# Attention prologue of a fused two-layer transformer kernel: fewer scores among the query/key blocks, the second stack's transfers interleaved, the last output tile in two halves

## The chip, the cores and the metric

One core of a Trainium2 chip runs the whole program. The metric is the device time of one execution in microseconds (us). Five things work side by side on a core: TensorE (PE in the profile; PEld is its loading of weights), VectorE (DVE), ScalarE (ACT), GpSimd (POOL) and SyncE (SP), whose queue here issues every transfer (SPq). They meet only at semaphores, and each does its instructions in program order. A median moved by under 0.2% can't be told from no change here.

## What is computed

Two blocks over 1024 tokens of width 512. The first (a state-space scan and a routed feed-forward) isn't touched. The second is attention with 32 heads of width 16 and a linear position bias, and a gated feed-forward with ternary weights. What matters, cut from the reference:

```
qkv = hidden_states @ w_attn + b_attn            # 1024 x 1536
scores = einsum('bqhd,bkhd->bhqk', q, k) * SCALE
scores = where(causal, scores + bias, -inf)
attn = softmax(scores)
out = einsum('bhqk,bkhd->bqhd', attn, v) @ w_proj + b_proj
...
inter = silu(gate) * up;  inter_q = trunc(clip(inter * 128, -128, 127))
down = einsum('bsi,hi->bsh', inter_q, w_down)
out = trunc(clip(down * 128, -128, 127));  x = x + gb * out
```

## The kernel before, in words

**Heads and stacks.** The heads go in eight groups of four. Queries and keys are computed in float32 and split into three bfloat16 parts each. A *stack* of a group holds these parts, and rows for the bias, one above the other, so that one bfloat16 matmul gives the exact score. There are three stack buffers; group g lies in `stack[g % 3]`.

**Query/key blocks.** `QK_ORDER` lists 16 blocks of 128 channels by 512 tokens. For block i TensorE does four float32 matmuls (L1123; the profile has two records for each), ScalarE copies the result to `qkf` (L746), VectorE makes the three parts `qkp` in four instructions (L1550 to L1553), and SP writes them to DRAM (`parts_dram`, L383). `qkp` has three buffers, so VectorE's block i waits for the write of block i-3. `qkf` has two.

**Loads of stacks.** `load_stack(g)` issues 14 loads: two for each of the six entries of TERMS (queries and keys) and two of position rows (`alibi`). All are issued by the helper at L321. SP issues stack 0 right after the write of block 4, once the writes of blocks 0 to 4 have landed, and stack 1 in one go after the write of block 6. The write of block 7 stands behind it in SP's queue. Blocks 0 to 4 hold all that both stacks need.

**Scores and maxima.** Before the softmax each row's extreme is found. `scores(n)` on TensorE makes one PSUM bank of scores (L1065: four heads of a 128x128 tile in four matmuls; L1068: one head by 512 keys). `maximum(n)` on VectorE reduces it to `mrow`: four masked reductions L1506 where the tile lies on the diagonal, otherwise one instruction, L1510 or L1513. The banks form a ring of three: score n waits until the maximum of the entry three before it is done. A group has 36 of them (SU). Scores run 48 (S_PRO) ahead of the attention loop, and these first 48 are made in two places: behind the last query/key blocks (`s_early(i)` says how many are done after block i), and between the steps of the values' projection (`s_steps(t, k)`). That projection, the V phase below, has 8 tiles of 4 steps, each step one matmul (two records of L1140). At the first score VectorE also copies a mask, `negT` (L1501), for which score 2 waits.

**The shift.** When group 0's 36 maxima are in, VectorE joins them (`rr`), GpSimd splits the result into parts (`rp`), TensorE transposes it (L1049, just before score 40), VectorE casts it (L1528) and SP loads it as three rows into the stack (`stack<-r`). `transposed_scores(0)`, the loop's first product (L1081), waits for these rows.

**The attention loop.** 288 steps, each with a score 48 ahead, a transposed score (L1081), ScalarE's exponential and, seven steps behind, the product with the values (L1101).

**The last stage.** The down projection has eight tiles of 128 tokens by 512 columns, 33 bfloat16 matmuls each (L1250). For a tile VectorE does nine dependent instructions (L1612, L1613, L1590 to L1593, L1595, L1616, L1618), ScalarE one (L807), and SP writes the tile out (L417). No other work is left then.

Of the kernel before, what the change touches and what calls it, by code (L numbers as in the profile page):

```python
# [29 lines left out]
EPS = 1e-5  # L30
QK_ORDER = ((0, 0), (4, 0), (1, 0), (0, 1), (4, 1), (5, 0), (1, 1), (5, 1),
            (2, 0), (6, 0), (3, 0), (7, 0), (2, 1), (6, 1), (3, 1), (7, 1))
S_QK = 9
QK_FIRST = 2
LEAD = 12
PV_LAG = 7
MAGIC = 12582912.0
HIGH = 3e38
TERMS = ((0, 0), (1, 0), (2, 0), (0, 1), (1, 1), (0, 2))
ATT_R = 3  # L40
ATT_A = 24
# [41 lines left out]
S_PRO = SU + LEAD  # L83
# [14 lines left out]
def program(nc, a, out):  # L98
    ctx = ExitStack()
    with ctx:  # L100
# [7 lines left out]
        x_tok = at("x_tok", 0, [P, NT, D])  # L108
# [91 lines left out]
        stack = [at("stack0", G_AT + 54, [P, 2, GH, T], BF16), at("stack1", F_AT + 22, [P, 2, GH, T], BF16),  # L200
                 at("stack2", G_AT + 32, [P, 2, GH, T], BF16)]
# [54 lines left out]
        def tile(t):  # L256
            return slice(t * P, (t + 1) * P)


        def s_early(i):  # L260
            return 0 if i < S_QK else (3 * (i - S_QK) + 4) // 2

        def s_steps(t, k):

            early = s_early(15)
            return early + (S_PRO - early) * (t * DC + k + 1) // (NT * DC)

        def qk_bank(i):
            return i if i < 4 else 4 + i % 4
# [49 lines left out]
        def _(sp):  # L319
            def load(dst, src, s):  # L320
                sp.dma_start(dst, src).then_inc(s, 16)  # L321
# [45 lines left out]
            load(bv[:], a["b_v"], S["bias1"])  # L367
            load(bpc[:], a["b_proj"].partition_broadcast(P), S["bias1"])

            def load_stack(g):  # L370
                def rows(part, first):
                    at_ = first + g * GH * HD
                    return parts_dram[part, at_:at_ + GH * HD, :].rearrange("(d h) t -> d (h t)", h=GH)

                for n, (qp, kp) in enumerate(TERMS):
                    load(stack[g % 3][n:ATT_K:ATT_W, 0, :, :], rows(qp, 0), stk[g % 3])
                    load(stack[g % 3][n:ATT_K:ATT_W, 1, :, :], rows(kp, D), stk[g % 3])
                load(stack[g % 3][ATT_W - 1:ATT_K:ATT_W, 1, :, :].bitcast(U16), a["alibi"][g][0:HD], stk[g % 3])
                load(stack[g % 3][ATT_K:ATT_S, 1, :, :].bitcast(U16), a["alibi"][g][HD:ATT_A], stk[g % 3])

            for i, (ob, h) in enumerate(QK_ORDER):
                sp.wait_ge(S["qk_split"], i + 1)
                sp.dma_start(parts_dram[:, ob * P:(ob + 1) * P, half(h)].rearrange("q p t -> p q t"), qkp[:, i % 3, :, :]) \  # L383
                  .then_inc(qk_wr[i % 3], 16)
                if i == 4:
                    for r in range(3):
                        sp.wait_ge(qk_wr[r], 16 * (2 if r < 2 else 1))
                    load_stack(0)
                if i == 6:
                    load_stack(1)  # L390
            for i in range(3):
                sp.wait_ge(qk_wr[i], 16 * len(range(i, 16, 3)))

# [18 lines left out]
            sp.wait_ge(S["ao_done"], 2 * NG)  # L412
            load(wd[:, 0:IC - 1, :], a["wd"][0:(IC - 1) * P, :].rearrange("(k p) n -> p k n", p=P), S["in_down"])
            load(wd[0:INTER - (IC - 1) * P, IC - 1, :], a["wd"][(IC - 1) * P:INTER, :], S["in_down"])
            for t in range(NT):
                sp.wait_ge(S["dn_done"], t + 1)
                sp.dma_start(out[tile(t), :], x_tok[:, t, :]).then_inc(S["out_dma"], 16)  # L417
            sp.wait_ge(S["out_dma"], 16 * NT)


        @block.gpsimd
# [114 lines left out]
        def _(act):  # L536
            n = [0]
# [6 lines left out]
            A_ = act.activation  # L544
# [214 lines left out]
            for F in range(NG * FU):  # L759
                g, f = F // FU, F % FU  # L760
# [5 lines left out]
                if on:  # L766
                    x = ps[:, 3 + F % 3, :].rearrange("p (n c) -> p n c", c=P)[:, on[0]:on[1] + 1:on[1] - on[0], :]
# [10 lines left out]
            for i in range(2 * IC):  # L778
                if i == 1:
                    ln_out(3, 1, 3, 4, (1,))  # L780
                ib, s = i % IC, i % 2
                M = min(P, INTER - ib * P)

                for part in range(3):
                    k = i - part
# [14 lines left out]
                if i >= 2:  # L800
                    act.wait_ge(S["f_out"], i - 1)
                A_(f_s[0:M, s, :], f_y[0:M, s, :], ACT.Sign).then_inc(S["f_sgn"], 1)
            for t in range(NT):
                act.wait_ge(S["dn_y0"], t + 1)
                if t >= 2:
                    act.wait_ge(S["dn_y"], t - 1)
                A_(f_s[:, t % 2, :], f_y[:, t % 2, :], ACT.Sign).then_inc(S["dn_sgn"], 1)  # L807


        @block.tensor  # L810
        def _(pe):
            mm = pe.matmul
# [156 lines left out]
            for m in range(N_ALL):  # L969
                h, s = m // NS, m % NS  # L970
# [143 lines left out]
            n = 0  # L1114
            for i, (ob, h) in enumerate(QK_ORDER):
# [18 lines left out]
            for t in range(NT):  # L1134
# [57 lines left out]
            for F in range(NG * FU):  # L1192
                g, f = F // FU, F % FU
# [34 lines left out]
            for i in range(2 * IC):  # L1228
# [3 lines left out]
                h, ib, s = i // IC, i % IC, i % 2  # L1232
                M = M_of(i)
# [9 lines left out]
            for t in range(NT):  # L1243
                pe.wait_ge(S["f_out"], IC * (t // 4 + 1))
                if t >= 4:
                    pe.wait_ge(S["dn_y"], t - 3)
                for k in range(IC):
                    M = M_of(k)
                    for part in range(3):
                        ins = mm(ps[:, 4 + t % 4, :], inter[0:M, k, tile(t)], wdp[0:M, part, k, :],  # L1250
                                 start=(k == 0 and part == 0), stop=(k == IC - 1 and part == 2))
                ins.then_inc(S["dn_mm"], 1)

# [2 lines left out]
        def _(v):  # L1256
            n = [0]

            def link(ins):
                n[0] += 1  # L1260
                ins.then_inc(S["dchain"], 1)
                v.wait_ge(S["dchain"], n[0])

            ts, tt, stt = v.tensor_scalar, v.tensor_tensor, v.scalar_tensor_tensor
# [323 lines left out]
            def trunc(y, s, M, sgn_sem, sgn_count, dst):

                link(ts(f_a[0:M, s, :].bitcast(I32), y.bitcast(I32), 0x7FFFFFFF, None, ALU.bitwise_and))  # L1590
                link(ts(f_m[0:M, s, :], f_a[0:M, s, :], MAGIC, None, ALU.add))
                link(stt(f_a[0:M, s, :], f_m[0:M, s, :], MAGIC, f_a[0:M, s, :], ALU.subtract, ALU.subtract))
                link(stt(f_m[0:M, s, :], f_a[0:M, s, :], 0.0, f_m[0:M, s, :], ALU.is_gt, ALU.subtract))  # L1593
                v.wait_ge(sgn_sem, sgn_count)
                return stt(dst, f_m[0:M, s, :], MAGIC, f_s[0:M, s, :], ALU.add, ALU.mult)  # L1595

            for i in range(2 * IC):
                h, ib, s = i // IC, i % IC, i % 2
# [9 lines left out]
            for t in range(NT):  # L1608
                s = t % 2
                v.wait_ge(S["dn_mm"], t + 1)  # L1610

                link(ts(f_y[:, s, :], ps[:, 4 + t % 4, :], -128.0, -128.0, ALU.mult, ALU.max))  # L1612
                ts(f_y[:, s, :], f_y[:, s, :], 127.0, None, ALU.min).then_inc(S["dn_y0"], 1)  # L1613
                v.wait_ge(S["dn_y0"], t + 1)
                link(trunc(f_y[:, s, :], s, P, S["dn_sgn"], t + 1, f_r[:, s, :]))
                tt(f_r[:, s, :], f_r[:, s, :], gb1[:], ALU.mult).then_inc(S["dn_y"], 1)  # L1616
                v.wait_ge(S["dn_y"], t + 1)
                tt(x_tok[:, t, :], x_tok[:, t, :], f_r[:, s, :], ALU.subtract).then_inc(S["dn_done"], 1)  # L1618
# [82 lines left out]
```

## Time and profile before

| | us |
|---|---|
| median of 3 runs | 903.29 (902.1 to 904.23) |
| the profiled execution, its own time | 903.27 |
| its span in the profile | 901.5 |
| PE busy | 850.0 (94%) |
| DVE busy | 742.8 (82%) |
| ACT busy | 472.0 (52%) |
| POOL busy | 308.9 (34%) |

The span is what the profile's records cover; the time is 1.77 us longer. Busy times of PE are sums of modelled lengths: a matmul's record is longer than the distance to the next, so the distance between two starts tells what one costs. The stage around the change runs from about 325 us (first query/key block) to 428 us (start of the attention loop); the last stage from 836 us to the end.

### The profile page before, as it was taken

The numbers are of one execution on the slowest core, as the hardware profiler recorded it, in microseconds if no ns is written. First come the engines' busy times: TensorE is split into PE (matmuls) and PEld (weight loads), VectorE is DVE, ScalarE is ACT, GpSimd is POOL, SyncE is SP. The second block draws the span as 40 slices with busy tenths as digits, with TensorE's granted clock in tenths as the row PEclk, the third lists the DMA queues.
The fourth block names the chain that finished last, engine by engine and source line by source line (L and its number), as shares of the span: only waits on it lengthen the run. The fifth ranks groups of instructions, "written<-read, shape, count | busy, mean of one in ns | idle before, by whom it ended". The sixth has DMA issues, their size and how long they took to land.

```text
span 901.5 us, 12080 instructions
## 1 busy us (share of the span) xinstructions
PE 850.0 (94%) x4031; PEld 401.3 (45%) x4031; DVE 742.8 (82%) x1589; ACT 472.0 (52%) x904; POOL 308.9 (34%) x342
## 2 busy tenths in 40 slices
PE   5999978999989999899999999999999999999996
PEld 3445424455437454444444444443344444444442
DVE  5689999999997875787999999995156899767777
ACT  4767654665652031111888888888624656333100
POOL 1057999999993100050122212212111433000000
PEclk9878999999999999999999999999999999999998
DMA  9300060300005005610322202200051000000011
GB/s 345 113 0 1 1 275 5 140 1 1 1 0 202 8 29 160 201 61 2 89 81 81 59 27 79 82 3 2 1 199 53 1 0 0 1 0 1 12 43 39
DMA packets 22136, 54.07 MB, mean 60 GB/s; under 512 B 6085, under 2 KB 12869, under 8 KB 19066
## 3 DMA queue, kind: packets, MB, share of 16 engines
q1 hardware_dynamic: 22074, 53.30, 17.1%
q8 instruction: 32, 0.52, 0.2%
q14 instruction: 30, 0.25, 0.1%
HBM read 44.70 MB, written 8.39 MB: 59 GB/s over the span
## 4 chain that ended last, share of the span: by engine, by line
PE 62%; DVE 4%; SPq 2%; POOL 1%; ACT 1%; issue 1%; DMA 1%; POOLq 0%; DVEq 0%
PE ps L1239 17%; PE ps L1101 8%; PE ps L1081 7%; PE ps L1250 6%; PE ps L1065 4%; PE ps L1068 4%; PE ps L1160 3%; PE ps L1009 3%; PE ps L1140 3%; PE ps L1123 2%; SPq L321 2%; PE ps L818 1%; POOL hC L482 1%; PE ps L1003 1%; PE ps L1110 1%
## 5 line engine op out<-in xcount | busy, mean ns | idle before, releaser
L482 POOL TENSOR_TENSOR hC<-hs,C_sb 128x512 f32<-128x512 f32 x128 | 160.7, 1274 | 51.4 <-ACT C_sb L701 30.7
L771 ACT ACTIVATE prob<-ps 128x512 f32<-128x512 f32 x288 | 157.8, 602 | 25.8 <-PE ps L1081 11.5
L989 PE MATMUL ps<-hC,identf 128*128 128x512 f32 x256 | 139.7, 650 | 13.2 <-POOL hC L482 12.2
L630 ACT ACTIVATE ps<-dtT,nA 128x512 f32<-128x512 f32 x128 | 88.2, 690 | 50.1 <-DVE hs L1394 46.6
L1081 PE MATMUL ps<-stack 123*128 123x512 bf16 (+3 forms) x384 | 108.5, 327 | 1.3 <-ACT prob L771 1.1
L520 POOL TENSOR_SCALAR_AFFINE_SELECT prob<-prob 128x256 f32<-128x256 f32 x96 | 39.2, 409 | 162.8 <-ACT prob L771 162.8
L1513 DVE TENSOR_REDUCE mrow<-ps 128x1 f32<-128x512 f32 x128 | 81.7, 682 | 6.3 <-PE ps L1068 4.3
L1101 PE MATMUL ps<-prob,V 128*32 128x512 f32 (+3 forms) x768 | 81.6, 498 | 0.7 <-POOL prob L520 0.7
L989 PEld LDWEIGHTS ps<-hC,identf 128*128 128x128 f32 x256 | 48.5, 204 | 72.8 <-POOL hC L482 53.1
L1239 PE MATMUL ps<-hT,wg 128*128 128x512 f32 (+1 forms) x176 | 79.1, 592 | 0.0
L1239 PE MATMUL ps<-hT,wu 128*128 128x512 f32 (+1 forms) x176 | 79.1, 592 | 0.0
L1394 DVE TENSOR_TENSOR_SCAN hs<-ps,dBx 128x512 f32<-128x512 f32 x64 | 77.7, 1214 | 1.2 <-ACT ps L630 1.2
L1372 DVE TENSOR_TENSOR dBx<-uT,ps 128x512 f32<-128x512 f32 x112 | 74.0, 662 | 3.8 <-PE ps L883 3.5
L1394 DVE TENSOR_TENSOR_SCAN hs<-ps,state,dBx 128x512 f32<-128x512 f32 x56 | 69.9, 1270 | 0.3 <-ACT ps L630 0.3
L1506 DVE CUSTOM_DVE_ANT_0 ps<-ps,negT 128x128 f32<-128x128 f32 x256 | 66.0, 321 | 3.3 <-PE ps L1065 2.0
L1510 DVE TENSOR_REDUCE mrow<-ps 128x4 f32<-128x512 f32 x96 | 63.2, 684 | 5.3 <-PE ps L1065 4.9
L1065 PEld LDWEIGHTS ps<-stack 120*128 120x128 bf16 x640 | 44.5, 97 | 48.6 <-issue 22.2
L1065 PE MATMUL ps<-stack 120*128 120x128 bf16 x640 | 61.6, 219 | 2.7 <-DVE mrow L1506 1.5
L1250 PE MATMUL ps<-wdp,inter 128*128 128x512 bf16 (+1 forms) x264 | 57.2, 379 | 0.0
L1123 PE MATMUL ps<-hT,wattn 128*128 128x512 f32 x128 | 56.6, 595 | 0.0
L1239 PEld LDWEIGHTS ps<-hT,wu 128*128 128x128 f32 (+1 forms) x176 | 33.0, 188 | 42.5 <-issue 42.5
L1239 PEld LDWEIGHTS ps<-hT,wg 128*128 128x128 f32 (+1 forms) x176 | 32.9, 188 | 42.0 <-issue 42.0
(202 smaller groups left out, 1334.8 us busy)
## 6 DMA issues: line engine op xcount, KB each, us to landing
stack<-parts_dram SPq DMA_DIRECT2D x96, 128.0 KB
wmod<-in_wmod SPq DMA_DIRECT2D x4, 1536.0 KB, 12.4
parts_dram<-qkp SPq DMA_DIRECT2D x16, 384.0 KB, 2.6
wmod<-in_wmod SPq DMA_DIRECT2D x4, 1024.0 KB, 10.5
wattn<-in_wattn SPq DMA_DIRECT2D x1, 3072.0 KB, 10.1
wg<-in_wg SPq DMA_DIRECT2D x1, 2752.0 KB, 11.0
wu<-in_wu SPq DMA_DIRECT2D x1, 2752.0 KB, 10.7
wd<-in_wd SPq DMA_DIRECT2D x1, 2560.0 KB, 11.1
```

Of the source, the lines that this page charges most:

```text
L482: pool.tensor_tensor(hC[:, c, :], hs[:, c, :], C_sb[:, m % 2, :], ALU.mult).then_inc(S["hc_done"], 1)
L630: A_(ps[:, DA_BANK + c % 2, :], dtT[:, c, half(h)], ACT.Exp, scale=nA[:, c * NS + s:c * NS + s + 1]).then_inc(S["da_done"], 1)
L771: A_(prob[:, u % 4, j, :], ps[:, 3 + F % 3, :], ACT.Exp, scale=-1.0).then_inc(S["exp_done"], 1)
L989: mm(ps[:, c, :], identf[:], hC[:, c, :], start=False, stop=(s == NS - 1), skip_group_check=True).then_inc(S["sum_done"], 1)
L1065: ins = mm(ps[:, bank, tile(j_)], qk[0:ATT_S, 0, j_, tile(i)], qk[0:ATT_S, 1, j_, tile(kb)], start=True, stop=True)
L1081: ins = mm(ps[:, bank, col:col + w], qk[0:ATT_ALL, 1, j, tile(kb)], qk[0:ATT_ALL, 0, j, q0:q0 + w], start=True, stop=not diag)
L1101: ins = mm(ps[32 * j:32 * j + 32, 6 + b, q0 % HALF:q0 % HALF + w], V[:, kb, g * GH + j, :], prob[:, U % 4, j, col:col + w], start=(kb == 0 ...
L1123: ins = mm(ps[:, qk_bank(i), :], wattn[:, k, ob * P:(ob + 1) * P], hT[:, k, half(h)], start=(k == 0), stop=(k == DC - 1))
L1239: ins = mm(ps[0:M, 2 * s + b, :], w[:, k, ib * P:ib * P + M], hT[:, k, half(h)], start=(k == 0), stop=(k == DC - 1))
L1250: ins = mm(ps[:, 4 + t % 4, :], inter[0:M, k, tile(t)], wdp[0:M, part, k, :], start=(k == 0 and part == 0), stop=(k == IC - 1 and part == 2))
L1394: v.tensor_tensor_scan(hs[:, c, :], ps[:, DA_BANK + c % 2, :], dBx[:, c, :] if c < mine else dB3[m % 2], init, ALU.mult, ALU.add).then_inc ...
L1513: v.tensor_reduce(mrow[:, 0, j, i:i + 1], ps[:, bank, :], AX, ALU.min).then_inc(S["m_done"], 1)
```

## The change

Three edits.

1. `S_QK` goes from 9 to 10 and `s_early` from (3(i-9)+4)/2 to i+1-10. After blocks 9 to 15 there used to be 2, 3, 5, 6, 8, 9 and 11 scores; now there are 0, 1, 2, 3, 4, 5 and 6. The five others go to the V phase: `s_steps` now gives no score after its first three steps (`V_AHEAD = 3`) and spreads 42 over the other 29, where it spread 37 over 32.
2. Stack 1 isn't loaded in one go after the write of block 6. Two of its loads follow each of the writes of blocks 6 to 12.
3. The last tile of the down projection is done as two halves of 256 columns, through all engines, to the write of the output.

```diff
-S_QK = 9
+S_QK = 10
+V_AHEAD = 3
...
+DOWN = [(t, 0, D) for t in range(NT - 1)] + [(NT - 1, 0, D // 2), (NT - 1, D // 2, D // 2)]
...
         def s_early(i):
-            return 0 if i < S_QK else (3 * (i - S_QK) + 4) // 2
+            return max(0, i + 1 - S_QK)
 
         def s_steps(t, k):
 
             early = s_early(15)
-            return early + (S_PRO - early) * (t * DC + k + 1) // (NT * DC)
+            return early + (S_PRO - early) * max(0, t * DC + k + 1 - V_AHEAD) // (NT * DC - V_AHEAD)
...
-                if i == 6:
-                    load_stack(1)
+                if 6 <= i < 6 + ATT_W:
+                    load_rows_of(1, i - 6)
...
-            for t in range(NT):
-                sp.wait_ge(S["dn_done"], t + 1)
-                sp.dma_start(out[tile(t), :], x_tok[:, t, :]).then_inc(S["out_dma"], 16)
+            for n, (t, c0, w) in enumerate(DOWN):
+                sp.wait_ge(S["dn_done"], n + 1)
+                sp.dma_start(out[tile(t), c0:c0 + w], x_tok[:, t, c0:c0 + w]).then_inc(S["out_dma"], 16)
...
-            for t in range(NT):
+            for n, (t, c0, w) in enumerate(DOWN):
                 pe.wait_ge(S["f_out"], IC * (t // 4 + 1))
-                if t >= 4:
-                    pe.wait_ge(S["dn_y"], t - 3)
+                if n >= 4:
+                    pe.wait_ge(S["dn_y"], n - 3)
                 for k in range(IC):
                     M = M_of(k)
                     for part in range(3):
-                        ins = mm(ps[:, 4 + t % 4, :], inter[0:M, k, tile(t)], wdp[0:M, part, k, :],
+                        ins = mm(ps[:, 4 + n % 4, 0:w], inter[0:M, k, tile(t)], wdp[0:M, part, k, c0:c0 + w],
                                  start=(k == 0 and part == 0), stop=(k == IC - 1 and part == 2))
...
-                link(ts(f_y[:, s, :], ps[:, 4 + t % 4, :], -128.0, -128.0, ALU.mult, ALU.max))
+                link(ts(y, ps[:, 4 + n_ % 4, 0:w], -128.0, -128.0, ALU.mult, ALU.max))
...
```

`load_rows_of(1, n)` issues the two loads of entry n, for n = 6 those of the position rows; `load_stack(g)` is now a loop over it. ScalarE's sign and VectorE's nine instructions of the down tiles get the width `w` in the same way.

How the instructions move. On TensorE, from the tenth query/key block to the fourth score of the V phase, before (in the kernel before L1123 is a query/key block, L1065 and L1068 scores, L1140 the V phase):

```order
L1123 MATMUL ps<-hT,wattn 128x512 x32
L1129 MATMUL ps<-identb,negm 128x128
L1065 MATMUL ps<-stack_126 128x128 x8
L1123 MATMUL ps<-hT,wattn 128x512 x4
L1065 MATMUL ps<-stack_126 128x128 x4
L1123 MATMUL ps<-hT,wattn 128x512 x4
L1065 MATMUL ps<-stack_126 128x128 x8
...
L1065 MATMUL ps<-stack_126 128x128 x8
L1140 MATMUL ps<-wattn,hT 128x512
L1068 MATMUL ps<-stack_126 128x512
L1140 MATMUL ps<-wattn,hT 128x512
L1068 MATMUL ps<-stack_126 128x512
```

And now (L1132 is the block, L1074 and L1077 the scores, L1149 the V phase):

```order
L1132 MATMUL ps<-hT,wattn 128x512 x36
L1138 MATMUL ps<-identb,negm 128x128
L1074 MATMUL ps<-stack_126 128x128 x4
L1132 MATMUL ps<-hT,wattn 128x512 x4
L1074 MATMUL ps<-stack_126 128x128 x4
L1132 MATMUL ps<-hT,wattn 128x512 x4
...
L1074 MATMUL ps<-stack_126 128x128 x4
L1149 MATMUL ps<-wattn,hT 128x512 x4
L1074 MATMUL ps<-stack_126 128x128 x4
L1149 MATMUL ps<-wattn,hT 128x512
L1074 MATMUL ps<-stack_126 128x128 x4
```

The first scores come one block later and singly, and four steps of the V phase go ahead of its first score. On SP, the transfers behind the load of stack 0 (stack_127 is stack 1), before:

```order
L383 DMA parts_dram<-qkp 128x3x512 x2
L321 DMA stack_127<-parts_dram 16x4096 x12
L321 DMA stack_127<-in_alibi 16x4096
L321 DMA stack_127<-in_alibi 8x4096
L383 DMA parts_dram<-qkp 128x3x512 x9
```

And now:

```order
L392 DMA parts_dram<-qkp 128x3x512 x2
L324 DMA stack_127<-parts_dram 16x4096 x2
L392 DMA parts_dram<-qkp 128x3x512
L324 DMA stack_127<-parts_dram 16x4096 x2
L392 DMA parts_dram<-qkp 128x3x512
...
L324 DMA stack_127<-parts_dram 16x4096 x2
L392 DMA parts_dram<-qkp 128x3x512
L324 DMA stack_127<-in_alibi 16x4096
L324 DMA stack_127<-in_alibi 8x4096
L392 DMA parts_dram<-qkp 128x3x512 x3
```

The write of block 7 stands behind two loads, where it stood behind fourteen.

## Rows read from the trace of the kernel before

**Rows 1.** Busy us by stretch (PE, PEld, DVE, ACT, POOL, clock, DMA): V phase; loop

```profile
387.90:427.00 39.10, 37.09 (x164) 17.37 (x162) 32.42 (x109) 4.64 (x9) 14.20 (x13) 1.00 0.07 21
456.00:484.40 28.40, 28.40 (x258) 13.15 (x257) 27.11 (x99) 24.06 (x50) 5.82 (x17) 1.00 0.22 65
```

**Rows 2.** Timeline, PE, query/key blocks: start, length, instruction, idle before it

```profile
361.81 3.65 PE L1123 MATMUL ps<-hT,wattn 128*128 128x512 f32 x8
366.69 0.40 PE L1065 MATMUL ps<-stack 120*128 120x128 bf16 x4 [1.23 <-DVE negT L1501]
366.93 3.65 PE L1123 MATMUL ps<-hT,wattn 128*128 128x512 f32 x8
370.42 0.61 PE L1065 MATMUL ps<-stack 120*128 120x128 bf16 x8
370.87 3.65 PE L1123 MATMUL ps<-hT,wattn 128*128 128x512 f32 x8
376.02 0.40 PE L1065 MATMUL ps<-stack 120*128 120x128 bf16 x4 [1.51 <-DVE mrow L1506]
```

**Rows 3.** Timeline, PE, V phase, its start and its end

```profile
387.85 1.08 PE L1140 MATMUL ps<-wattn,hT 128*128 128x512 f32 x2
388.91 0.39 PE L1068 MATMUL ps<-stack 120*128 120x512 bf16 x1
389.14 1.02 PE L1140 MATMUL ps<-wattn,hT 128*128 128x512 f32 x2
392.17 0.39 PE L1068 MATMUL ps<-stack 120*128 120x512 bf16 x1 [2.01 <-DVE mrow L1506]
...
426.96 0.38 PE L1068 MATMUL ps<-stack 120*128 120x512 bf16 x1
```

**Rows 4.** Timeline, DVE, first instructions of blocks 8 and 10

```profile
361.85 0.43 DVE L1550 CAST qkp<-qkf 128x512 bf16<-128x512 f32 x1 [4.19 <-DMA parts_dram<-qkp]
...
372.62 0.43 DVE L1550 CAST qkp<-qkf 128x512 bf16<-128x512 f32 x1 [4.30 <-DMA parts_dram<-qkp]
```

**Rows 5.** Timeline, SP's queue, around the loads of stack 1

```profile
358.95 0.90 SPq L383 DMA_DIRECT2D parts_dram<-qkp  x2
359.89 8.13 SPq L321 DMA_DIRECT2D stack<-parts_dram  x12
...
369.22 22.27 SPq L383 DMA_DIRECT2D parts_dram<-qkp  x9
```

**Rows 6.** Timeline, DVE, V phase: a diagonal maximum's start, then three others

```profile
403.85 0.30 DVE L1506 CUSTOM_DVE_ANT_0 ps<-ps,negT 128x128 f32<-128x128 f32 x1 [0.45 <-PE ps L1065]
...
404.98 1.99 DVE L1513 TENSOR_REDUCE mrow<-ps 128x1 f32<-128x512 f32 x3
```

**Rows 7.** Timeline, PE and SP: the shift of group 0, and the loop's first product

```profile
419.66 0.22 PE L1049 MATMUL ps<-identb,rp 128*96 128x128 bf16 x1
...
420.84 1.81 SPq L321 DMA_DIRECT2D stack<-r  x3
...
427.81 0.38 PE L1081 MATMUL ps<-stack 123*128 123x512 bf16 x1
```

**Rows 8.** Timeline, PE and DVE, last stage: tile 6's last instruction, tile 7's

```profile
836.19 57.17 PE L1250 MATMUL ps<-wdp,inter 128*128 128x512 bf16 x264
...
891.28 0.69 DVE L1618 TENSOR_TENSOR x_tok<-x_tok,f_r 128x512 f32<-128x512 f32 x1
893.40 0.69 DVE L1612 TENSOR_SCALAR f_y<-ps 128x512 f32<-128x512 f32 x1 [1.42 <-PE ps L1250]
894.12 0.43 DVE L1613 TENSOR_SCALAR f_y<-f_y 128x512 f32<-128x512 f32 x1
...
898.41 0.69 DVE L1618 TENSOR_TENSOR x_tok<-x_tok,f_r 128x512 f32<-128x512 f32 x1
```

**Rows 9.** Groups by form, DVE, width 256: one slow and one fast form

```profile
L1540 DVE TENSOR_TENSOR AO<-ps,rec 128x256 f32<-128x256 f32 x16 | 6.8, 425 | 0.6
L1492 DVE MEMSET mrow<- 128x256 f32 x1 | 0.3, 272 | 0.0
```

More of the change, by code:

```diff
@@ L368, in _, with load_rows_of @@
             load(bpc[:], a["b_proj"].partition_broadcast(P), S["bias1"])
-            def load_stack(g):
+            def load_rows_of(g, n):
                 def rows(part, first):
@@ L373, in rows, with load_stack @@
                     return parts_dram[part, at_:at_ + GH * HD, :].rearrange("(d h) t -> d (h t)", h=GH)
-                for n, (qp, kp) in enumerate(TERMS):
+                if n < len(TERMS):
+                    qp, kp = TERMS[n]
                     load(stack[g % 3][n:ATT_K:ATT_W, 0, :, :], rows(qp, 0), stk[g % 3])
                     load(stack[g % 3][n:ATT_K:ATT_W, 1, :, :], rows(kp, D), stk[g % 3])
-                load(stack[g % 3][ATT_W - 1:ATT_K:ATT_W, 1, :, :].bitcast(U16), a["alibi"][g][0:HD], stk[g % 3])
-                load(stack[g % 3][ATT_K:ATT_S, 1, :, :].bitcast(U16), a["alibi"][g][HD:ATT_A], stk[g % 3])
+                else:
+                    load(stack[g % 3][ATT_W - 1:ATT_K:ATT_W, 1, :, :].bitcast(U16), a["alibi"][g][0:HD], stk[g % 3])
+                    load(stack[g % 3][ATT_K:ATT_S, 1, :, :].bitcast(U16), a["alibi"][g][HD:ATT_A], stk[g % 3])
+            def load_stack(g):
+                for n in range(ATT_W):
+                    load_rows_of(g, n)
             for i, (ob, h) in enumerate(QK_ORDER):
@@ L414, in _ @@
             load(wd[0:INTER - (IC - 1) * P, IC - 1, :], a["wd"][(IC - 1) * P:INTER, :], S["in_down"])
-            for t in range(NT):
-                sp.wait_ge(S["dn_done"], t + 1)
-                sp.dma_start(out[tile(t), :], x_tok[:, t, :]).then_inc(S["out_dma"], 16)
-            sp.wait_ge(S["out_dma"], 16 * NT)
+            for n, (t, c0, w) in enumerate(DOWN):
+                sp.wait_ge(S["dn_done"], n + 1)
+                sp.dma_start(out[tile(t), c0:c0 + w], x_tok[:, t, c0:c0 + w]).then_inc(S["out_dma"], 16)
+            sp.wait_ge(S["out_dma"], 16 * len(DOWN))
         @block.gpsimd
@@ L802, in _ @@
                 A_(f_s[0:M, s, :], f_y[0:M, s, :], ACT.Sign).then_inc(S["f_sgn"], 1)
-            for t in range(NT):
[L804 to L807, printed above, removed]
+            for n_, (t, c0, w) in enumerate(DOWN):
+                act.wait_ge(S["dn_y0"], n_ + 1)
+                if n_ >= 2:
+                    act.wait_ge(S["dn_y"], n_ - 1)
+                A_(f_s[:, n_ % 2, 0:w], f_y[:, n_ % 2, 0:w], ACT.Sign).then_inc(S["dn_sgn"], 1)
         @block.tensor
@@ L1242, in _ @@
             pe.wait_ge(S["wd_p2"], IC)
-            for t in range(NT):
+            for n, (t, c0, w) in enumerate(DOWN):
                 pe.wait_ge(S["f_out"], IC * (t // 4 + 1))
-                if t >= 4:
-                    pe.wait_ge(S["dn_y"], t - 3)
+                if n >= 4:
+                    pe.wait_ge(S["dn_y"], n - 3)
                 for k in range(IC):
@@ L1586, in _, with trunc @@
             ln_norm(3, 1)
[L1588 to L1593, printed above, removed]
+            def trunc(y, s, M, sgn_sem, sgn_count, dst, w=HALF):
+                a_, m_ = f_a[0:M, s, 0:w], f_m[0:M, s, 0:w]
+                link(ts(a_.bitcast(I32), y.bitcast(I32), 0x7FFFFFFF, None, ALU.bitwise_and))
+                link(ts(m_, a_, MAGIC, None, ALU.add))
+                link(stt(a_, m_, MAGIC, a_, ALU.subtract, ALU.subtract))
+                link(stt(m_, a_, 0.0, m_, ALU.is_gt, ALU.subtract))
                 v.wait_ge(sgn_sem, sgn_count)
-                return stt(dst, f_m[0:M, s, :], MAGIC, f_s[0:M, s, :], ALU.add, ALU.mult)
+                return stt(dst, m_, MAGIC, f_s[0:M, s, 0:w], ALU.add, ALU.mult)
             for i in range(2 * IC):
@@ L1607, in _ @@
                 trunc(f_y[0:M, s, :], s, M, S["f_sgn"], i + 1, inter[0:M, ib, half(h)]).then_inc(S["f_out"], 1)
-            for t in range(NT):
-                s = t % 2
-                v.wait_ge(S["dn_mm"], t + 1)
-                link(ts(f_y[:, s, :], ps[:, 4 + t % 4, :], -128.0, -128.0, ALU.mult, ALU.max))
[L1613 to L1618, printed above, removed]
+            for n_, (t, c0, w) in enumerate(DOWN):
+                s = n_ % 2
+                v.wait_ge(S["dn_mm"], n_ + 1)
+                y, r, x = f_y[:, s, 0:w], f_r[:, s, 0:w], x_tok[:, t, c0:c0 + w]
+                link(ts(y, ps[:, 4 + n_ % 4, 0:w], -128.0, -128.0, ALU.mult, ALU.max))
+                ts(y, y, 127.0, None, ALU.min).then_inc(S["dn_y0"], 1)
+                v.wait_ge(S["dn_y0"], n_ + 1)
+                link(trunc(y, s, P, S["dn_sgn"], n_ + 1, r, w))
+                tt(r, r, gb1[:, c0:c0 + w], ALU.mult).then_inc(S["dn_y"], 1)
+                v.wait_ge(S["dn_y"], n_ + 1)
+                tt(x, x, r, ALU.subtract).then_inc(S["dn_done"], 1)
 def bf16_bits(x):
```

## The prediction

> **What bounds the kernel.** I read the busy time by stretch first. In the attention loop TensorE is busy for all of a group's 28.40 us, VectorE for 27.11 [rows 1]. TensorE is the bound there with 1.29 us of VectorE to spare, and the change adds no work to the loop. In the V phase before it TensorE has gaps, and VectorE is busy for 32.42 of 39.10 us. So I read TensorE's timeline from block 10 to the end of the V phase, and look at distances between starts. A block followed by its score costs 3.49 us (366.93 to 370.42). Block 10 takes 4.88 (361.81 to 366.69) and block 12 takes 5.15 (370.87 to 376.02): 1.39 and 1.66 too much [rows 2]. A V step alone costs 0.86 (two of 0.43; 392.17 + 0.22 for the score is where the next begins). The first takes 1.06 and the second 3.03 (389.14 to 392.17): 0.20 and 2.17 too much [rows 3]. Together TensorE loses **5.42 us** in four places. All wait for VectorE: for the mask's copy, or for a maximum that frees a bank of the ring.
>
> Why is VectorE late? It stands still for 4.19 us before block 8 and 4.30 before block 10 [rows 4], for a write of `qkp`. SP's queue shows which. Write 5 goes out at 358.95, behind stack 0, and has landed at 361.85 (2.9 us). Write 7 goes out at 369.22, behind stack 1's fourteen loads, and has landed at 372.62 (3.4 us) [rows 4, 5]. The maxima stand behind block 10's four instructions in VectorE's program, so the scores' banks stay full. Afterwards VectorE catches up through the rest of the blocks, with 11 maxima among them.
>
> **The transfers.** Stack 0 stays, so block 8 still starts at 361.85. Writes 5 and 6 end at 359.89 as before. Then two loads at 0.68 each (8.13 for twelve) and write 7 is issued at about 361.25, 8 us earlier. Landed after 2.9 to 3.4 us, it is there by 364.7. VectorE does blocks 8 and 9 at 2.25 each (0.43 + 0.69 + 0.43 + 0.69 a block) until 366.35, so block 10 finds its buffer free. Later writes go out when their block is split (block 8: 364.1) and are wanted three blocks later: write 8 by block 11 at about 369.9. SP needs 1.36 for a pair and 0.45 for a write, of about 3.7 between blocks, so nothing queues up. The last pair goes out near 376; score 36, its first reader, comes past 410. **The 4.30 us of rows 4 go; the 4.19 stay**, hidden by the block that TensorE now does before its first score. The number of transfers is the same, so is their cost to SP.
>
> **The scores.** TensorE, from 361.26 (end of block 9): block 10 takes 3.43, the mask's matmul 0.09, then five times a score (0.22) and a block (3.49), and score 5. That is 3.43 + 0.09 + 5 x 3.71 + 0.22 = 22.3: the V phase starts at **383.6**, not 387.85. VectorE does block 10 until 368.6, then the mask (0.31) and maximum 0 (0.97), to 369.9. Each later block has 2.25 plus one maximum of 0.6 to 1.0, at most 3.3 of TensorE's 3.7. Score 2, which wants the mask, comes at about 372, and the ring's waits are two blocks away. I expect no wait of TensorE here.
>
> The V phase now holds 32 x 0.86 for steps, 42 x 0.22 for scores, 0.22 for the shift, and 0.05 extra for some 19 steps that follow a four-matmul score (27.5 + 9.2 + 0.2 + 0.95 = 37.9). It ends at **421.5**, not at 427.2 (426.96 + 0.22) [rows 3]. The five scores moved cost the same 1.1 us in either place. VectorE's share: ten diagonal maxima at 1.13 (403.85 to 404.98), 32 others at 0.60 (1.99 for three less the overlap) [rows 6], and some 1.2 for joins and casts, 31.7 of 37.9 us. That fits on average. The scores now come in twos in nearly every second gap, and around the group's edge (scores 36 to 46, five of them diagonal) VectorE has some 9.4 us of work where TensorE has 9.2; the ring's three banks take up most of that. The three steps without a score let maximum 5, which comes after block 15's split at 386.6, finish by 387.7, before score 8 wants its bank near 389.4. I put 0.2 us on what is left: **5.42 - 0.2 = 5.2 us gained**. From the other side 427.2 - 421.5 = 5.7 less 0.2 is 5.5; I take the lower. Bounds: 5.8 (no new wait, every small gap closed) and 3.0 (both crowded places cost their full excess, below).
>
> **The shift.** It comes relatively later: behind it lie four V steps and eight scores (5.4 us), where six steps lay. From the transpose at 419.66 to the last issue at 422.65 are 3.0 us, and with 2.9 for landing (write 5's) 5.9 [rows 7]. The loop's first product came 8.15 after the transpose; now about 6.3. Spare 0.4, so nothing, but thinly.
>
> **The last tile.** TensorE's last matmul ends at 893.38, and a tile takes 57.17/8 = 7.15. The first half would be ready at about 889.8. But VectorE is busy with tile 6 until 891.28 + 0.60 = 891.88 [rows 8], and so **the halves don't start early by the whole 3.6 us**. A half is nine instructions of width 256. Six are slow (0.69 at 512; 0.425 at 256), three fast (0.43; 0.272) [rows 8, 9]; with 0.03 between dependent ones 6 x 0.46 + 3 x 0.30 = 3.66. First half: 891.88 to 895.4. The second was ready at 893.4, starts at 895.4 and ends at 899.05. Before, the chain ended at 898.41 + 0.69 = 899.10. The eighteen short instructions eat what the early start gives. Then the output's landing, now 2.4 (to 901.5), of half the bytes: I take 0.1 less. **Together 0.15 us gained.** Bounds: instructions exactly half as long end at 897.5 (1.6 gained); fast ones that don't shrink, as the three times 0.16 twice, cost 1.0. TensorE's 66 short matmuls have 2.3 us of cover (895.4 against 893.4, and 891.88 against 889.8).
>
> The Trainium skill (DMA: Bandwidth & Descriptors, section "Anatomy of one DMA — SWDGE (gpsimd) path") puts a transfer at a fixed 2.0 us plus its bytes at 436 GB/s. By it 128 KB less save 0.3 us, and the sum would be 0.2 lower; its fit is for another issuing path.
>
> **Sum.** 903.27 - 5.2 - 0.15 = **897.9 us**. The profiled execution stands at the median (903.29), so this is the median too. Everything behind the V phase hangs on semaphores, not on a fixed time, so the shift is carried to the end.
>
> **Rivals.**
> - *VectorE can't keep up in the V phase.* If reductions cost 0.69 and the diagonal 1.13 in the crowd, scores 36 to 46 with joins take 10.7 us against 9.2, and the first scores lose some 0.8: 2.3 us given back, 900.2. For it: 42 scores in 29 steps. Against: VectorE waited for TensorE 0.4 us at nearly every score [rows 6]. Chance 0.10.
> - *The writes land behind the pairs.* A write that lands more than 5.1 us after its issue holds up VectorE again, once or twice, for about 1.5 us: 899.4. Against: 3.4 us even behind fourteen loads [rows 4, 5]. Chance 0.05. The Trainium skill speaks for this one (same page, "Queues, rings and completion order"): a transfer's semaphore increment lands only after every earlier write of that DMA engine. The trace agrees in sign only, 3.4 against 2.9.
> - *Short instructions aren't shorter* in the last tile: twice 5.7 from 891.9 end at 903.3, 4.1 later, and 902.1 comes out. Rows 9 speak against it. Chance 0.02.
> - *Nothing is gained.* The removed waits were beside a longer chain, or scores wait as long in the V phase as they did before: about 903.1. Against: no other engine is busy enough there [rows 1]. Chance 0.03.
> - *Slower: VectorE becomes the loop's bound.* Its 27.11 us count reductions that overlap at 0.60. If the loop is entered so that each starts from a standstill (0.69), 28 a group add 2.5, 29.6 against 28.40, or 1.2 in each of seven groups: +8.4 less 5.35 is +3, **906.3**. It decides once VectorE needs over 28.40 a group. Against: the last five scores before the loop stand as they did, so its entry should look alike. Chance 0.04.
>
> **How the numbers follow.** The forecast has 0.76. Its own spread, 5.2 (4.3 to 5.8) and 0.15 (-0.6 to 0.9), gives 896.6 to 899.5. I widen to 896.2 at the fast end, for the last tile's bound, and to 900.2 for the crowded V phase. Left out are the last three rivals (0.09) and the edges. A change under 0.2% (1.8 us) can't be told from none. Faster by more: 0.76 + 0.10 + 0.05 = 0.91. Within: 0.02 + 0.03 = 0.05. Slower: 0.04.
>
> **What would show it.** No wait of VectorE before block 10, one of 4.2 before block 8. TensorE's blocks at 3.49 with a score each, the V phase from 383.6 to 421.5, waits in it under 0.5 us together. Loop groups of 28.40. VectorE's last nine instructions at 0.425 and 0.27, starting near 895.4 - 5.2 = 890.2. It is wrong if the V phase shows waits over 2 us, if the loop's first product waits for the `r` rows, or if groups take longer.

## The result, and the profile after

| | before | changed |
|---|---|---|
| median | 903.29 (902.1 to 904.23, 4 runs) | 897.74 (897.41 to 899.48, 4 runs) |
| ratio | | 0.9938 (0.9924 to 0.9952) |
| profiled execution, time / span | 903.27 / 901.5 | 899.48 / 897.8 |

The changed kernel is 5.5 us faster, which is 0.6%. The forecast was 897.9. The profiled execution of the changed kernel is its slowest: it reached the first query/key block 1.68 us later (326.86 against 325.18), before anything that the change touches. So the stages are compared by distances between two instructions, not by times from the start of the span. Two distances do: *the prologue*, from TensorE's first matmul of block 0 to the loop's first product, and *the last stage's end*, from the first instruction on tile 6 after TensorE's end of it to VectorE's last. Their starts, before and in the changed kernel, and the changed kernel's first matmul of the last stage (that of before is in [rows 8], the loop's first product of before in [rows 7]):

```profile
325.18 7.03 PE L1123 MATMUL ps<-hT,wattn 128*128 128x512 f32 x16
886.27 0.69 DVE L1612 TENSOR_SCALAR f_y<-ps 128x512 f32<-128x512 f32 x1 [1.42 <-PE ps L1250]
...
326.86 3.60 PE L1132 MATMUL ps<-hT,wattn 128*128 128x512 f32 x8
832.59 57.26 PE L1259 MATMUL ps<-wdp,inter 128*128 128x512 bf16 x297
```

| | before | changed | forecast |
|---|---|---|---|
| prologue | 102.63 | 97.34 | 5.2 less |
| loop's first product to the last stage's first matmul | 408.38 | 408.39 | the same |
| last stage's end | 12.83 | 12.94 | 0.05 less |
| VectorE's last instruction to the end of the span | 2.40 | 2.18 | 0.1 less |

The distances give 5.39 us together, the medians 5.55. The granted clock of TensorE was 1.00 in both prologues, so the clock has no part in their 5.29 us.

The timeline of TensorE in the changed kernel, for [rows 2, 3] (start, length, instruction, idle before it):

```profile
366.38 0.22 PE L1138 MATMUL ps<-identb,negm 128*128 128x128 bf16 x1
366.44 0.39 PE L1074 MATMUL ps<-stack 120*128 120x128 bf16 x4
366.66 3.65 PE L1132 MATMUL ps<-hT,wattn 128*128 128x512 f32 x8
370.15 0.39 PE L1074 MATMUL ps<-stack 120*128 120x128 bf16 x4
...
385.01 0.39 PE L1074 MATMUL ps<-stack 120*128 120x128 bf16 x4
385.23 3.65 PE L1149 MATMUL ps<-wattn,hT 128*128 128x512 f32 x8
...
417.64 0.22 PE L1058 MATMUL ps<-identb,rp 128*96 128x128 bf16 x1
417.79 0.94 PE L1074 MATMUL ps<-stack 120*128 120x128 bf16 x8
418.57 1.08 PE L1149 MATMUL ps<-wattn,hT 128*128 128x512 f32 x2
...
423.98 0.39 PE L1077 MATMUL ps<-stack 120*128 120x512 bf16 x1 [0.25 <-ACT V L760]
424.20 0.38 PE L1090 MATMUL ps<-stack 123*128 123x512 bf16 x1
```

No row of the blocks or of the V phase carries a wait. A block with its score is 3.71 (366.44 to 370.15), the 3.49 and 0.22 of the working. The V phase starts at 385.23, which is 383.55 in the time of the kernel before. The one new wait is at the shift: the pair of scores behind it takes 0.78 (417.79 to 418.57), where a pair takes 0.45 elsewhere, so 0.33 is lost. The 0.25 before the loop was there before. From the transpose to the loop's first product are 6.56 us (417.64 to 424.20), and no row shows the product waiting.

VectorE and SP's queue in the changed kernel, for [rows 4, 5]:

```profile
363.74 0.43 DVE L1559 CAST qkp<-qkf 128x512 bf16<-128x512 f32 x1 [4.40 <-DMA parts_dram<-qkp]
...
366.00 0.42 DVE L1559 CAST qkp<-qkf 128x512 bf16<-128x512 f32 x1
...
368.25 0.42 DVE L1559 CAST qkp<-qkf 128x512 bf16<-128x512 f32 x1
```

```profile
360.63 0.91 SPq L392 DMA_DIRECT2D parts_dram<-qkp  x2
361.58 1.88 SPq L324 DMA_DIRECT2D stack<-parts_dram  x2
363.50 0.58 SPq L392 DMA_DIRECT2D parts_dram<-qkp  x1
364.12 1.13 SPq L324 DMA_DIRECT2D stack<-parts_dram  x2
366.11 0.37 SPq L392 DMA_DIRECT2D parts_dram<-qkp  x1
```

Blocks 8, 9 and 10 follow one another at 2.25: the wait before block 8 stayed and the one before block 10 is gone. The first pair took SP 1.88, not 1.36, and write 7 still went out 4.75 us before VectorE wanted its buffer (368.25: the start of block 10).

The end, for [rows 8, 9]: VectorE's timeline of the changed kernel, the second half after the last instruction of the first.

```profile
882.68 0.69 DVE L1621 TENSOR_SCALAR f_y<-ps 128x512 f32<-128x512 f32 x1 [1.42 <-PE ps L1259]
...
888.30 0.42 DVE L1621 TENSOR_SCALAR f_y<-ps 128x256 f32<-128x256 f32 x1
888.75 0.29 DVE L1622 TENSOR_SCALAR f_y<-f_y 128x256 f32<-128x256 f32 x1
...
891.92 0.42 DVE L1621 TENSOR_SCALAR f_y<-ps 128x256 f32<-128x256 f32 x1
...
895.20 0.42 DVE L1627 TENSOR_TENSOR x_tok<-x_tok,f_r 128x256 f32<-128x256 f32 x1
```

The first half starts 0.61 after tile 6's last instruction has started (887.69), without a wait, and a half takes 3.62 (888.30 to 891.92), where 3.66 was worked out for nine dependent instructions. As worked out, the early start buys nothing.

### The profile page after: what moved, and what is told of

The parts are those of the page before. It is cut to its first block, busy times and chain, and to the rows that moved or that the text cites. A ratio compares the mean times of both kernels' runs of the same rounds, so it can differ in the third digit from the quotient of the medians.

```text
span 897.8 us, 12160 instructions
## 1 busy us (share of the span) xinstructions
PE 851.6 (95%) x4064; PEld 407.5 (45%) x4064; DVE 743.9 (83%) x1598; ACT 472.3 (53%) x905; POOL 308.4 (34%) x342
## 4 chain that ended last, share of the span: by engine, by line
PE 66%; DVE 3%; POOL 1%; ACT 1%; issue 0%; POOLq 0%
PE ps L1248 17%; PE ps L1110 8%; PE ps L1090 7%; PE ps L1132 6%; PE ps L1259 6%; PE ps L1074 4%; PE ps L1077 4%; PE ps L1169 3%; PE ps L1018 3%; PE ps L1149 3%; PE ps L827 1%; POOL hC L491 1%; PE ps L1012 1%; PE ps L1119 1%; PE ps L1021 1%; PE ps L1164 0%
## 5 line engine op out<-in xcount | busy, mean ns | idle before, releaser
L1074 PEld LDWEIGHTS ps<-stack 120*128 120x128 bf16 x640 | 44.5, 97 | 44.5 <-issue 21.7
L1074 PE MATMUL ps<-stack 120*128 120x128 bf16 x640 | 61.4, 219 | 0.1
L1259 PE MATMUL ps<-wdp,inter 128*128 128x512 bf16 (+3 forms) x297 | 57.3, 355 | 0.0
L1132 PE MATMUL ps<-hT,wattn 128*128 128x512 f32 x128 | 56.4, 594 | 0.0
```

Source lines behind the costliest of these rows:

```text
L1074: ins = mm(ps[:, bank, tile(j_)], qk[0:ATT_S, 0, j_, tile(i)], qk[0:ATT_S, 1, j_, tile(kb)], start=True, stop=True)
L1259: ins = mm(ps[:, 4 + n % 4, 0:w], inter[0:M, k, tile(t)], wdp[0:M, part, k, c0:c0 + w], start=(k == 0 and part == 0), stop=(k == IC - 1 an ...
```

## The experiments

The theory: TensorE lost 5.4 us in the prologue because VectorE was late with maxima; it was late because a write stood behind fourteen loads, and because scores stood too early and too close. Both edits are then needed, and the halves do nothing since VectorE, not TensorE, ends the last stage. The rivals give the whole gain to one edit, or some of it to the halves. The ratios below are to the kernel before, run beside each experiment, with their 95% intervals.

**Each edit alone.** e1 takes `s_early` and `s_steps` of the change and leaves the rest:

```diff
 # e1, against the changed kernel
-                if 6 <= i < 6 + ATT_W:
-                    load_rows_of(1, i - 6)
+                if i == 6:
+                    load_stack(1)
-DOWN = [(t, 0, D) for t in range(NT - 1)] + [(NT - 1, 0, D // 2), (NT - 1, D // 2, D // 2)]
+DOWN = [(t, 0, D) for t in range(NT)]
```

> Only the new places of the scores; stack 1 is loaded in one go after write 6, the last tile is whole. Measured from the start of query/key block 0 to the loop's first product: 102.6 us before, 97.3 with the whole change. Theory (both edits are needed: write 7 behind fourteen loads makes VectorE late, and the scores stand behind it): VectorE waits 4.2 us before block 10 as before, the mask comes at about 372.6 of the kernel before, and since now score 2 comes a block later TensorE waits for it only there, about 3.7 us in one place, none in the V phase: about 101.0 us for the stretch, 901.6 us in all. Rival (the places of the scores are the whole gain): 97.3 for the stretch, 898 in all, no wait for the mask.

Measured: 901.39, ratio 0.9976 (0.9964 to 0.9988), prologue 100.30 (325.24 to 425.54). TensorE and VectorE in its timeline:

```profile
368.75 3.65 PE L1132 MATMUL ps<-hT,wattn 128*128 128x512 f32 x8
375.18 0.40 PE L1074 MATMUL ps<-stack 120*128 120x128 bf16 x4 [2.77 <-DVE negT L1510]
```

```profile
372.58 0.43 DVE L1559 CAST qkp<-qkf 128x512 bf16<-128x512 f32 x1 [6.00 <-DMA parts_dram<-qkp]
```

One wait, at score 2 and for the mask, as expected; by starts it is 6.43 - 3.49 = 2.94, not 3.7. VectorE starts block 10 at 372.58, where [rows 4] have 372.62. So 2.33 of the 5.29 us come from the scores' places alone, and the rest hangs on the write.

e2 keeps the loads two by two and puts the scores back:

```diff
 # e2, against the changed kernel; and the last tile whole
-S_QK = 10
-V_AHEAD = 3
+S_QK = 9
+V_AHEAD = 0
-            return max(0, i + 1 - S_QK)
+            return 0 if i < S_QK else (3 * (i - S_QK) + 4) // 2
```

> Only stack 1's loads two by two; scores and last tile as in the kernel before. Theory: VectorE no longer waits before block 10, but two scores already stand after block 9, whose mask and maxima queue on VectorE behind the blocks it is late with after write 5: TensorE still waits 1.2 to 1.4 us for the mask and about 1.8 us at score 12 in the V phase; about 100.1 us for the stretch from block 0 to the loop's first product, some 900.8 us in all. Rival (the transfers are the whole gain): 97.3 for the stretch, 898 in all.

Measured: 901.52, 0.9978 (0.9966 to 0.999), prologue 100.84 (324.85 to 425.69). TensorE's timeline:

```profile
361.61 3.65 PE L1132 MATMUL ps<-hT,wattn 128*128 128x512 f32 x8
366.69 0.40 PE L1074 MATMUL ps<-stack 120*128 120x128 bf16 x4 [1.43 <-DVE negT L1510]
...
387.30 1.02 PE L1149 MATMUL ps<-wattn,hT 128*128 128x512 f32 x2
390.05 0.39 PE L1077 MATMUL ps<-stack 120*128 120x512 bf16 x1 [1.73 <-DVE mrow L1515]
```

The second of the four waits, at score 5 [rows 2], is gone, and the small third with it (the V phase's first step takes 0.91, not 1.06). The mask's is by starts 1.59 and the one in the V phase 1.89. The waits are the expected ones, the total was set 0.7 too low. The loads alone bring 1.79 us. Alone the two edits make 4.12, together 5.29: each leaves a wait that only the other takes away. Both rivals fall: neither edit alone comes near a prologue of 97.3.

e3 has the halves alone (`S_QK = 9`, the old `s_early`, `V_AHEAD = 0`, stack 1 in one go), e5 everything but the halves:

> Only the last tile in halves. Theory: VectorE is still busy with tile 6 when the first half is ready, and eighteen instructions of 256 cost as much as the early start gives: from the start of the last stage's matmuls to VectorE's last instruction 62.9 us as before, within 0.2, and the output lands 0.2 sooner: no difference in the time (903.2). Rival (the half that is ready 3.6 us early is what counts): the last instruction ends 1.6 us or more sooner, 901.6.

> The change without its third edit: scores and transfers as in the changed kernel, last tile whole. Theory: 97.3 us from block 0's start to the loop's first product, from TensorE's end of tile 6 to VectorE's last instruction 12.85, the output's landing 0.2 longer: the time of the changed kernel within 0.3 us (897.9). Rival (the halves carry some of the gain): 899 or more.

Measured: e3 903.94, 1.0003 (0.9994 to 1.0012), last stage's end 12.93 (887.37 to 900.30), then 2.1 to the end of the span. e5 898.23, 0.9951 (0.9935 to 0.9967), prologue 97.35, last stage's end 12.83 (881.70 to 894.53), then 2.47. The halves cost VectorE 0.1 and save the output 0.3 or so. Nothing is left that the medians could show, with either prologue.

**The three steps without a score.** e4 sets `V_AHEAD = 0` in the changed kernel.

> The whole change, but scores start after the first step of the V phase (V_AHEAD = 0). Theory: VectorE still has block 15's split, maximum 5 and the bias's product to do when scores 6 to 8 come, so TensorE waits 0.8 us at score 8 and 0.4 at 10: the stretch is 98.2 us instead of 97.3, 898.6 in all. Rival (the ring of three banks takes it up): 97.3, no wait.

Measured: 899.45, 0.995 (0.9932 to 0.9969), prologue 98.47 (326.33 to 424.80). Its waits of TensorE in the prologue (engine, line, waited for: us in total, times, longest):

```profile
PE ps L1074 <- DVE mrow L1515: 0.7, 1, 0.7
PE ps L1077 <- ACT V L760: 0.2, 1, 0.2
PE ps L1074 <- DVE mrow L1519: 0.2, 1, 0.2
```

The waits come back where they were expected, at score 8 and score 10 (0.92 and 0.38 by starts, 0.8 and 0.4 expected); the one at the shift isn't there, and the prologue is 1.13 us longer than the changed kernel's. The ring of three banks doesn't absorb a maximum behind a block's split, the bias's product, and two more. The medians are too close to tell it apart; the trace does.

**Is two by two the point?** e6 puts four loads behind each of the writes of blocks 6 to 8 and two behind block 9's; e7 puts all fourteen behind the write of block 15.

```diff
 # e6
-                if 6 <= i < 6 + ATT_W:
-                    load_rows_of(1, i - 6)
+                if 6 <= i < 10:
+                    for n in range(2 * (i - 6), min(2 * (i - 6) + 2, ATT_W)):
+                        load_rows_of(1, n)
```

> The whole change, but stack 1's loads go four at a time behind the writes of blocks 6 to 8 and two behind block 9's. Theory (write 7 has about 5.1 us from its issue until VectorE wants its buffer, and lands in 2.9 to 3.4): two more loads put it off by about 1.2 us, it still lands in time: 97.3 us from block 0's start to the loop's first product, at most 0.3 more, VectorE waits for no write after block 8. Rival (two by two is as much as the queue bears; loads queued before a write add to its landing): VectorE waits over 1 us for write 7 or 8 and the stretch is 98.3 or more.

> The whole change, but all fourteen loads of stack 1 are issued behind the write of block 15. Theory (all that counts is that no write stands behind them; score 36, their first reader, comes only past 410 us): the stretch stays 97.3 us, write 7 lands even sooner. Rival (the loads gain by the blocks' time, and late ones are late for score 36 or collide with the V phase): TensorE waits for stack 1 before score 36, or the stretch is longer by 0.5 us or more.

Measured: prologue 97.35 in both (326.07 to 423.42; 325.34 to 422.69), times 898.68 and 897.98, one run each. SP's queue in e6 and in e7:

```profile
359.85 0.90 SPq L392 DMA_DIRECT2D parts_dram<-qkp  x2
360.79 3.04 SPq L324 DMA_DIRECT2D stack<-parts_dram  x4
363.87 0.58 SPq L392 DMA_DIRECT2D parts_dram<-qkp  x1
```

```profile
359.11 28.02 SPq L392 DMA_DIRECT2D parts_dram<-qkp  x11
387.18 7.47 SPq L324 DMA_DIRECT2D stack<-parts_dram  x12
394.68 1.11 SPq L324 DMA_DIRECT2D stack<-in_alibi  x2
```

In e6 write 7 goes out at 363.87 and VectorE isn't held up (block 9 starts at 365.39, block 10 at 367.65): there was room for twice as many loads. In e7 the first load of stack 1 goes out 61.8 us after the first query/key block, against 34.7 in the changed kernel, and nobody waits for it. So it is only that write 7 doesn't stand behind fourteen loads; between these three ways of dealing them out the prologue differs by 0.01 us.

**Can the last stage be shortened?** If VectorE's work sets its end, taking instructions off VectorE should show, and the halves should start to pay. e8 has GpSimd multiply the sign by the gate (what VectorE's last multiplication then writes is the same value, and its separate product falls away); e10 also has ScalarE scale by -128:

```diff
 # e8, GpSimd, behind its weights' loop
+            for n_, (t, c0, w) in enumerate(DOWN):
+                pool.wait_ge(S["dn_sgn"], n_ + 1)
+                pool.tensor_tensor(f_s[:, n_ % 2, 0:w], f_s[:, n_ % 2, 0:w], gb1[:, c0:c0 + w], ALU.mult) \
+                    .then_inc(S["dn_gs"], 1)
...
 # VectorE
-                link(trunc(y, s, P, S["dn_sgn"], n_ + 1, r, w))
-                tt(r, r, gb1[:, c0:c0 + w], ALU.mult).then_inc(S["dn_y"], 1)
+                trunc(y, s, P, S["dn_gs"], n_ + 1, r, w).then_inc(S["dn_y"], 1)
 # e10 besides: ScalarE, then VectorE
...
+                A_(f_y[:, n_ % 2, 0:w], ps[:, 4 + n_ % 4, 0:w], ACT.Copy, scale=-128.0).then_inc(S["dn_sc"], 1)
...
-                link(ts(y, ps[:, 4 + n_ % 4, 0:w], -128.0, -128.0, ALU.mult, ALU.max))
-                ts(y, y, 127.0, None, ALU.min).then_inc(S["dn_y0"], 1)
+                ts(y, y, -128.0, 127.0, ALU.max, ALU.min).then_inc(S["dn_y0"], 1)
```

> The whole change, and in the last stage GpSimd multiplies the sign by the gate while VectorE truncates, so that VectorE's last multiplication writes the gated value and its separate product falls away: eight instructions a tile, not nine. Theory (the last stage ends with VectorE's total work, not with TensorE): from VectorE's first instruction of tile 6 to its last of all 12.94 us now, less 0.72 for tile 6 and 0.46 for each half: 11.3; 1.65 us sooner, 896.1 in all. Rival (the second half waits for TensorE, whose last matmul comes 7.1 us after tile 6's start): 0.46 us sooner only, 12.5, 897.3; or GpSimd is too slow and the chain waits for it, no gain.

> As the one before, and ScalarE takes the scaling by -128 out of PSUM, so VectorE clamps in one fast instruction: seven a tile. Theory: ScalarE's copy (0.6, or 0.4 for a half) lies before each chain, but for the last half it runs while VectorE is at the first, so that VectorE is still nearly the bound: from TensorE's end of tile 6 to the last instruction 10.4 us, 2.5 sooner than with the change alone, 895.2 in all. Rival (the added step is in the chain): not sooner than the one before, 11.3.

Measured: e8 897.34, 0.9934 (0.9919 to 0.9949), last stage's end 13.07 (881.50 to 894.57), where 11.3 was expected. e10 896.71, 0.9923 (0.9906 to 0.9939), 12.06 (882.56 to 894.62), where 10.4 was. In e8 the saved instruction is gone from the timeline and no time with it. Tile 6 in e8, VectorE and GpSimd:

```profile
883.15 0.43 DVE L1604 TENSOR_SCALAR f_m<-f_a 128x512 f32<-128x512 f32 x1
883.40 1.30 POOL L544 TENSOR_TENSOR f_s<-f_s,gb 128x512 f32<-128x512 f32 x1 [5.82 <-ACT f_s L820]
883.62 1.64 DVE L1605 SCALAR_TENSOR_TENSOR f_a<-f_m,f_a 128x512 f32<-128x512 f32 x1
885.29 0.69 DVE L1606 SCALAR_TENSOR_TENSOR f_m<-f_a,f_m 128x512 f32<-128x512 f32 x1
```

The instruction that takes 0.69 [rows 8] takes 1.64 here. GpSimd ends at 884.70, VectorE at 885.26, 0.56 later. It isn't the wait for GpSimd's result: this instruction reads and writes only `f_m` and `f_a`, and the wait for `f_s` stands before L1608, two instructions on. In the last half the same instruction takes 0.84 for 0.42. I had counted GpSimd as idle and so as free; its product cost VectorE 0.95, more than the 0.72 of the instruction saved.

e11 leaves GpSimd out and keeps ScalarE's part, e12 does that with the last tile whole:

> The whole change, ScalarE takes the scaling by -128 out of PSUM, VectorE clamps in one instruction, and the gate's product stays on VectorE (GpSimd does nothing in the last stage). Theory (in the two runs before, VectorE's instruction with two operands in SBUF stood 0.95 us, or 0.42 for a half, because GpSimd's product ran beside it, and that ate the instruction saved; the stage itself ends with VectorE's total work): eight instructions a tile and no long one, from TensorE's end of tile 6 to VectorE's last 12.0 us against 12.96 with the change alone and 12.1 with both moves; 896.8 in all. Rival (instruction count is what matters, GpSimd is free): 0.46 us a half later than with both moves, 13.0.

> As the one before, but the last tile whole. Theory: without halves the chain of the last tile starts with TensorE's end of tile 7, 7.12 us after tile 6's, then 0.63 for ScalarE and 5.0 for eight instructions: 12.75 us from TensorE's end of tile 6. With the scaling moved, halves are worth 0.8 us, where they were worth nothing before, since tile 6 now leaves VectorE earlier. Rival (halves are worth nothing in any case, the short instructions eat them): the same as with halves within 0.2.

Measured: e11 896.93 (the kernel before gave 902.49 on this chip), 0.9935 (0.992 to 0.995), last stage's end **11.94** (881.14 to 893.08), 12.0 expected. e12 897.79, 0.9949 (0.993 to 0.9969), 12.73 (880.72 to 893.45), 12.75 expected. ScalarE and VectorE of e11:

```profile
881.14 0.60 ACT L818 ACTIVATE f_y<-ps 128x512 f32<-128x512 f32 x1 [5.41 <-PE ps L1263]
...
888.36 0.38 ACT L818 ACTIVATE f_y<-ps 128x256 f32<-128x256 f32 x1 [0.94 <-PE ps L1263]
```

```profile
883.16 0.69 DVE L1605 SCALAR_TENSOR_TENSOR f_a<-f_m,f_a 128x512 f32<-128x512 f32 x1
...
887.66 0.42 DVE L1605 SCALAR_TENSOR_TENSOR f_a<-f_m,f_a 128x256 f32<-128x256 f32 x1
...
889.84 0.29 DVE L1625 TENSOR_SCALAR f_y<-f_y 128x256 f32<-128x256 f32 x1
...
892.65 0.43 DVE L1630 TENSOR_TENSOR x_tok<-x_tok,f_r 128x256 f32<-128x256 f32 x1
```

In tile 6 the instruction at L1605 takes 0.69 here (883.16). ScalarE's copy for the second half (888.36) is done before VectorE is through with the first (889.84), and no instruction is long. With one move less than e10 it ends earlier. The halves now pay 0.8 us, 11.94 against 12.73. With the last tile in halves VectorE has no wait from tile 6 to its end, and one instruction less a tile makes it 1.0 us shorter (11.94 against 12.94): so VectorE's work is what ends the stage.

Why the halves pay here and not in the changed kernel can be read from VectorE's first instruction on the last tile and from its end. In e11 that first instruction comes 5.54 us after the first one on tile 6 (886.68) and in e12 7.76 (888.48), so halves start 2.22 earlier and then take 1.43 more (6.40 against 4.97). In the changed kernel against e5 it is 5.62 (888.30) against 7.12 (888.82), 1.50 earlier, and 1.61 more (7.32 against 5.71). Most of the difference is that a whole last tile now has ScalarE's copy ahead of it, which halves hide; that tile 6 leaves VectorE earlier, the reason given in the expectation of e12, is 0.08 of it. By the trace e11 is 1.0 us shorter there than the changed kernel; the ratios to the kernel before (0.9935 and 0.9938) can't tell the two apart, and so it isn't shown to beat it.

## Why the prediction was right

- **The waits of TensorE**, 5.42 us by distances between starts, less 0.2 of new ones: 5.29 came. All four went. Adding the idle times the trace prints (1.23, 1.51, 2.01) would have given 4.75; the distances were the better measure. That it came within 0.1 is in part luck, since two small errors cancel: the new wait was 0.33 and not 0.2, and about 0.2 of small gaps went as well that the four waits leave out (5.42 - 0.33 + 0.2 = 5.29). Some 0.15 of these lie ahead of the V phase, where single scores stand instead of pairs. The new wait was at the shift, where the working had put the crowd of scores 36 to 46; VectorE kept up elsewhere.
- **The transfers.** Right in mechanism: the wait before block 8 stays and does no harm, the one before block 10 goes (e1, e2). Write 7 had 4.75 us where 5.1 was worked out, because the first pair took SP longer. I had treated the dealing two by two as something to be costed; e6 and e7 show that with four loads before write 7, or none, the prologue is the same.
- **The V phase** ended at 421.9 in the time of the kernel before (423.35 + 0.22 - 1.68), 421.5 forecast; the new wait of 0.33 is most of the difference. The start, 383.55, was met.
- **The shift** had a spare of 0.4 in the working, and did not hold up the loop. The last issue came 2.74 after the transpose (418.56 + 1.82 against 417.64), where 3.0 was put.
- **The last tile**, 0.15 forecast and 0.11 found (0.11 lost by VectorE, 0.22 gained by the landing). That is luck: two terms were each a little off and the errors cancel, the last stage's end by 0.16, the landing by 0.12. The first is a slip in the working: from 891.88 a half of 3.66 ends at 895.54, not 895.4, and the second at 899.20, not 899.05, which is 0.10 later than before, as the trace shows it. Two other figures there are off without effect: 836.19 + 57.17 is 893.36, and the cover of TensorE's short matmuls is 2.0 by the times given, not 2.3. On the landing the rule of the Trainium skill (DMA: Bandwidth & Descriptors, "Anatomy of one DMA — SWDGE (gpsimd) path"), 0.3 less for 128 KB less, was nearer than my 0.1: the trace shows 0.22, and 2.47 against 2.18 between e5 and the changed kernel.
- **The rivals.** VectorE kept up in the V phase; the writes landed in time even behind four loads; the short instructions are short (0.42 and 0.29); something was gained; and the loop kept its 408.38 us from its first product to the last stage.
- What failed were expectations behind the prediction: e1 and e2 were off by 0.7 us in opposite directions, measured by the prologue. In e1 the cause stays open: write 7 landed as expected, and the expectation shows no working for its 3.7. In e2 some 0.4 of it is that I took idle times and not distances (1.3 + 1.8 against 1.59 + 1.89). e8 and e10 were off by 1.8 and 1.7, and the long instructions beside GpSimd's products are worth 0.95 + 0.42 + 0.42 = 1.79.

## What to carry to other kernels

Measure a stall by the distance between two starts against the undisturbed distance, follow it back through every queue, and ask for each edit what is left if it comes alone: here two edits of 2.3 and 1.8 us make 5.3 together. A queue of transfers is a program too: a write that someone waits for must not stand behind loads that nobody wants for another 40 us, and how those loads are spread made no difference in the three orders run here. Splitting the last tile pays by the earlier start, counted from when the engine behind the matmuls is through with the tile before, less what the shorter instructions cost in sum: 1.50 against 1.61 us in the changed kernel, 2.22 against 1.43 in e11.

## What the hardware showed that I had not expected

GpSimd and VectorE get in each other's way. A VectorE instruction with two operands in SBUF (0.69 at 128x512 f32) that met a GpSimd product of the same size (1.30) took 1.64, and ended 0.56 after GpSimd's; at width 256 it took 0.84 instead of 0.42 beside a product of 0.72. The trace has one record of 1.64 and no wait in it, so that VectorE stood still until GpSimd was through is read from the two ends, not shown. The single-operand one that GpSimd's product began beside (883.15) kept its 0.43. Without GpSimd's product (e11) it took 0.69 and 0.42. The Trainium skill says this (SBUF — State Buffer, "SBUF: two separate sides"): the two share a port pair, which is an exclusive lock held for a whole instruction, and a VectorE instruction with two SBUF inputs needs it against a GpSimd instruction that reads SBUF; these traces agree, with 1.64 for 0.69, and I should have looked before the run.
